# Cross-attention softmax sums: GpSimd adds seven of a head's eight probability chunks instead of six

## The chip, the cores and the metric

The kernel runs on one core of a Trainium2 chip. The metric is the device time of one execution in microseconds (us), as the median of several runs. Engines are named as in the profile: PE is TensorE's matmul queue and PEld its weight loads, DVE is VectorE, ACT is ScalarE, POOL is GpSimd, SP is SyncE, which issues most of the DMAs.

## The reference

Three layers follow each other: a cross-attention of 256 tokens over a context of 4096 rows, a causal self-attention, and a gated feed-forward network. Only the first matters here. It has 16 heads of 32 dimensions:

```python
q = _qdq(x) @ _qdq(wq).T + bq
kv = cond @ wkv.T + bkv
k, v = jnp.split(kv, 2, axis=-1)
# q, k, v reshaped to heads
attn = jax.nn.softmax(jnp.einsum('bnhd,bmhd->bhnm', q, k) * scale, axis=-1)
o = jnp.einsum('bhnm,bmhd->bnhd', attn, v).reshape(B, N, C)
out = _qdq(o) @ _qdq(wp).T + bp
```

So each head needs exponentials of 256 x 4096 scores, their product with V, and, for every token, the sum of its 4096 exponentials, by which the product is divided.

## The kernel before

The program first computes K and V of the context (up to about 207 us), then the 16 heads (to about 466 us), then the projection, the self-attention and the feed-forward network.

A head's 4096 context rows are cut into eight chunks (CHUNKS = 8) of 512. The probabilities of a chunk are stored transposed, context rows on the partitions, as 128 x 1024 float32: four blocks of 128 rows by 256 tokens. They stand in p_ring, which has four places; chunk c lies in place c % 4, so chunk c + 4 overwrites chunk c.

For each head h, the engines do this:

- PE, in `scores` (line 1347): four matmuls a chunk into a PSUM bank pair. Between them `maximum_pass` (line 1254) computes scores of the next head, of which VectorE takes row maxima (line 946).
- ACT, in `exponentials` (line 689): one exponential a chunk, from PSUM to p_ring.
- PE, in `values` (line 1359): the product of a chunk's probabilities with V, summed in bank 6 over the chunks.
- The sum over context rows: a product with a matrix of ones, `denominators` (line 1371), four matmuls into the other half of bank 6. It isn't made for every chunk. Chunks in SUM_CHUNKS are first added to each other elementwise, into p_sum, and one product with ones is made of the result. The others get their own.
- POOL, in `sum_chunks` (line 570), makes these additions for heads 0 to 14: the first adds chunks 0 and 1, each later one adds a chunk to p_sum. p_sum has two places, for even and odd heads. In head 15 DVE does them, in `add_last` (line 1034).
- After the last chunk, PE waits for all additions of the head, makes the product with ones of p_sum, and signals sums_used. ACT then copies bank 6 to o_t, in `evacuate_output` (line 678). `merge` on PE (lines 1333, 1335) and `normalize_output` on DVE divide.

Every engine works through its own queue in program order. The order around the change:

- PE, in `head(h)`, goes through four rounds: maxima, scores of two chunks, maxima, and then the values of the two chunks before these. In the first round of head h those are chunks 6 and 7 of head h - 1, and with chunk 7 comes the product of head h - 1's p_sum. `merge(h - 1)` stands in the second round.
- ACT makes exponential 0 of head h, then copies o_t for head h - 1, and then makes exponentials 1 to 7.

```python
for c in range(CHUNKS):
    if c == 1 and not first:
        evacuate_output(h - 1)           # waits for sums_used, line 677
    act.wait_ge(s_done, 8 * h + c + 1)
    wait(act, pv_done, 8 * h + c - 3)
    summed = SUMS_BEFORE[c]
    if summed is not None:
        wait(act, sums_done, NSUMS * h + summed)
```

SUMS_BEFORE[c] says how many additions, counted from the start of the head (NSUMS a head, negative for the head before), must be over before exponential c may overwrite its place in p_ring; None where the overwritten chunk isn't added. On PE:

```python
if c not in SUM_CHUNKS:
    last = denominators(p_ring[:, c % 4, :])
last.then_inc(pv_done, 1)
if c == CHUNKS - 1:
    pe.wait_ge(sums_done, NSUMS * h + NSUMS)
    denominators(p_sum[:, p, :]).then_inc(sums_used, 1)
```

Of the kernel before, what the change touches and what calls it, by code (L numbers as in the profile page):

```python
# [43 lines left out]
DH = D // H  # L44
HPG = P // DH
SPLIT_ROWS = 3 * DH
SUM_CHUNKS = (0, 1, 2, 4, 5, 6)
NSUMS = len(SUM_CHUNKS) - 1
SUMS_BEFORE = (-2, -1, 0, None, 1, 1, 2, None)
MAX_ROWS = 2  # L50
MT = M // P
CHUNKS = MT // 4
# [52 lines left out]
def wait(eng, sem, value):  # L105
    if positive(value):
        eng.wait_ge(sem, value)


def perceiver(nc, x_in, stream, wq_in, wp_in, bias_cols, bias_rows, out):  # L110
    with ExitStack() as ctx:
# [416 lines left out]
        def _(pool):  # L528
# [33 lines left out]
            def sum_chunks(h, p):  # L562

                for n, c in enumerate(SUM_CHUNKS[1:]):
                    pool.wait_ge(exp_done, 8 * h + c + 1)
# [44 lines left out]
        def _(act):  # L610
# [69 lines left out]
            def exponentials(h, first=False):  # L680
                for c in range(CHUNKS):
# [3 lines left out]
# [3 lines that stand above are left out]
# [173 lines left out]
        def _(dve):  # L861
# [165 lines left out]
            def add_last(n):  # L1027

                h, c = H - 1, SUM_CHUNKS[n + 1]
                dve.wait_ge(exp_done, 8 * h + c + 1)  # L1030
# [168 lines left out]
        def _(pe):  # L1199
# [152 lines left out]
            def values(h, p, loads, c):  # L1352
# [5 lines left out]
                for k in range(4):  # L1358
                    last = nc.tensor.matmul(bank(6)[k * DH:(k + 1) * DH, 0:N], v_head[p][:, 4 * c + k, :],  # L1359
                                            p_ring[:, c % 4, k * N:(k + 1) * N], start=c == 0, stop=c == CHUNKS - 1)  # L1360
                if c not in SUM_CHUNKS:
                    last = denominators(p_ring[:, c % 4, :])
# [5 lines left out]
            def denominators(probabilities):  # L1368

                for k in range(4):  # L1370
                    last = nc.tensor.matmul(bank(6)[k * DH:(k + 1) * DH, N:2 * N], ones_col[:],  # L1371
                                            probabilities[:, k * N:(k + 1) * N], start=False, stop=False,
                                            skip_group_check=True)
                return last
# [292 lines left out]
```

## Time and profile before

| | |
|---|---|
| median of 3 runs | 666.28 us (665.68 to 669.96) |
| the profiled execution | 667.73 us, span 665.9 us |
| PE busy | 618.1 us, 93% of the span |
| DVE busy | 372.9 us, 56% |
| ACT busy | 298.4 us, 45% |
| POOL busy | 228.2 us, 34% |
| mean granted TensorE clock | 0.972 of full speed |

The span is the time from the first to the last instruction of the profiled execution. Busy time of an engine is the time in which an instruction of it runs. The 34% of POOL lie mostly between 209 and 452 us; in the stretch before it does nearly nothing. In a timeline, a row can stand for several instructions in a row; its second number is then the time from the start of the first to the end of the last. A bracket gives the idle time of the engine before the row and what ended it.

### The profile page before, as it was taken

What the parts mean: (1) busy time and instruction counts of PE and PEld (TensorE: products, weight loads), DVE (VectorE), ACT (ScalarE), POOL (GpSimd) and SP (SyncE); (2) the same over time, 40 slices, a digit from 0 to 9 for tenths busy, and PEclk for the clock granted to TensorE, in tenths of its full rate; (3) what the DMA queues carried; (4) which work ended last, traced back from release to release, by engine and by line L of the source; (5) the groups of instructions that cost most, each with busy time, mean ns of one, the idle gap of its engine ahead of it and who ended that gap; (6) DMA issues with size and microseconds to landing.
All of it is one profiled execution on the core that took longest, in us unless ns stands there. A gap on an engine that the chain in (4) does not pass through costs nothing.

```text
span 665.9 us, 12397 instructions
## 1 busy us (share of the span) xinstructions
PE 618.1 (93%) x4340; PEld 478.0 (72%) x4340; DVE 372.9 (56%) x680; ACT 298.4 (45%) x424; POOL 228.2 (34%) x120
## 2 busy tenths in 40 slices
PE   5999999999998999999999999998499899979998
PEld 3877788888885666666666666665289788769997
DVE  3796530332237777777777777754555333365552
ACT  3444233133324444444555555554236676744441
POOL 1000200000024777767777777771100544320000
PEclk9999999999999999999999999997689799979999
DMA  8673644443386555555555555520022224135520
GB/s 305 231 242 126 200 147 167 157 161 120 127 253 178 139 140 138 138 138 138 138 138 138 138 138 142 143 79 1 0 83 109 85 105 189 65 120 186 184 81 32
DMA packets 29757, 92.17 MB, mean 138 GB/s; under 512 B 5472, under 2 KB 9568, under 8 KB 23008
## 3 DMA queue, kind: packets, MB, share of 16 engines
q1 hardware_dynamic: 28480, 89.67, 44.5%
q10 hardware_dynamic: 1248, 2.10, 0.8%
q8 instruction: 19, 0.31, 0.2%
q14 instruction: 10, 0.08, 0.0%
HBM read 65.02 MB, written 18.35 MB: 125 GB/s over the span
## 4 chain that ended last, share of the span: by engine, by line
PE 83%; ACT 6%; DVE 5%; issue 3%; DMA 2%; POOL 1%; SPq 0%; ACTq 0%; POOLq 0%; DVEq 0%
PE ps L333 16%; PE ps L334 15%; PE ps L335 15%; PE ps L1254 10%; PE ps L1359 9%; PE ps L1347 8%; PE ps L1371 3%; ACT p_ring L689 3%; POOL p_sum L570 1%; PE ps L1333 1%; PE ps L1335 1%; DMA f_ring<-stream 1%; DMA k_stack<-kh_scratch 1%; PE ps L1496 1%; PE ps L1325 1%
## 5 line engine op out<-in xcount | busy, mean ns | idle before, releaser
L946 DVE TENSOR_REDUCE m_part<-ps 128x1 f32<-128x512 f32 (+1 forms) x256 | 165.5, 686 | 93.0 <-PE ps L1254 87.4
L689 ACT ACTIVATE p_ring<-ps 128x1024 f32<-128x1024 f32 x128 | 124.6, 1024 | 100.9 <-PE ps L1347 100.9
L570 POOL TENSOR_TENSOR p_sum<-p_sum,p_ring 128x1024 f32<-128x1024 f32 x60 | 142.8, 2380 | 11.6 <-ACT p_ring L689 7.5
L1254 PE MATMUL ps<-k_stack,q_max 96*128 96x512 f32 (+1 forms) x256 | 98.3, 438 | 3.6 <-DVE m_part L946 1.3
L1347 PEld LDWEIGHTS ps<-q_stack,k_stack 98*128 98x128 f32 x512 | 71.2, 191 | 18.6 <-ACT p_ring L689 11.0
L1347 PE MATMUL ps<-q_stack,k_stack 98*128 98x256 f32 x512 | 77.0, 289 | 7.8 <-ACT p_ring L689 7.8
L1359 PE MATMUL ps<-p_ring,v_head 128*32 128x256 f32 x1024 | 75.4, 390 | 0.1
L1254 PEld LDWEIGHTS ps<-k_stack,q_max 96*128 96x128 f32 x256 | 42.6, 188 | 42.7 <-issue 21.2
L333 PE MATMUL ps<-xt_h,h_ring 128*128 128x256 f32 x208 | 61.0, 293 | 2.2 <-DVE xt_l L1060 2.2
L334 PE MATMUL ps<-xt_l,h_ring 128*128 128x256 f32 x208 | 60.5, 291 | 0.0
L335 PE MATMUL ps<-xt_h,l_ring 128*128 128x256 f32 x208 | 60.4, 290 | 0.0
L333 PE MATMUL ps<-h_ring,wkv_h 128*128 128x512 f32 x128 | 52.2, 408 | 8.5 <-DVE l_ring L866 8.1
L906 DVE SCALAR_TENSOR_TENSOR kl_buf<-ps,biases,kh_buf 128x512 fp32r<-128x512 f32 x32 | 23.9, 749 | 63.6 <-ACT kh_buf L647 63.3
L570 POOL TENSOR_TENSOR p_sum<-p_ring 128x1024 f32<-128x1024 f32 x15 | 35.6, 2372 | 67.8 <-ACT p_ring L689 67.8
L312 DVE TENSOR_TENSOR l_ring<-f_ring,h_ring 128x2048 fp32r<-128x2048 f32 x22 | 50.2, 2288 | 12.6 <-ACT h_ring L308 12.5
L334 PE MATMUL ps<-l_ring,wkv_h 128*128 128x512 f32 x128 | 51.5, 402 | 0.0
L335 PE MATMUL ps<-h_ring,wkv_l 128*128 128x512 f32 x128 | 51.5, 402 | 0.0
L333 PE MATMUL ps<-wkv_h,h_ring 128*128 128x512 f32 x128 | 50.8, 397 | 0.0
L335 PE MATMUL ps<-wkv_h,l_ring 128*128 128x512 f32 x128 | 50.6, 396 | 0.0
L334 PE MATMUL ps<-wkv_l,h_ring 128*128 128x512 f32 x128 | 50.6, 395 | 0.0
L661 ACT COPY v_all<-ps 128x512 f32 (+1 forms) x32 | 18.8, 587 | 69.3 <-PE ps L335 69.3
L647 ACT ACTIVATE kh_buf<-ps,biases 128x512 fp32r<-128x512 f32 x32 | 22.0, 688 | 57.2 <-PE ps L335 57.2
(183 smaller groups left out, 1016.6 us busy)
## 6 DMA issues: line engine op xcount, KB each, us to landing
f_ring<-stream SPq DMA_DIRECT2D x29, 1024.0 KB, 4.9
k_stack<-kh_scratch SPq DMA_DIRECT2D x60, 256.0 KB, 4.6
kh_scratch<-kh_buf SPq DMA_DIRECT2D x32, 256.0 KB, 5.5
kl_scratch<-kl_buf SPq DMA_DIRECT2D x32, 256.0 KB, 5.9
v_head<-v_all SPq DMA_DIRECT2D x16, 512.0 KB, 3.0
k_stack<-kl_scratch SPq DMA_DIRECT2D x30, 256.0 KB, 4.2
v_all<-stream SPq DMA_DIRECT2D x4, 256.0 KB, 4.7
f_ring<-stream SPq DMA_DIRECT2D x4, 256.0 KB, 5.7
```

The costliest lines, as they stand in the source:

```text
L312: nc.vector.tensor_tensor(l_ring[which][:], f_ring[which][:], h_ring[which][:].bitcast(F32), ALU.subtract).then_inc(l_ready, 1)
L333: nc.tensor.matmul(out_ap, lh, rh, start=start, stop=False)
L334: nc.tensor.matmul(out_ap, lh, rl, start=False, stop=False)
L335: return nc.tensor.matmul(out_ap, ll, rh, start=False, stop=stop)
L570: nc.gpsimd.tensor_tensor(p_sum[:, p, :], p_ring[:, 0, :] if n == 0 else p_sum[:, p, :], p_ring[:, c % 4, :], ALU.add).then_inc(sums_done, 1)
L647: nc.scalar.activation(kh_buf[:, g, :], bank(g % 2), ACT.Identity, bias=biases[:, KT + g:KT + g + 1]).then_inc(kh_evac, 1)
L689: nc.scalar.activation(p_ring[:, c % 4, :], ps[:, 2 * (c % 2):2 * (c % 2) + 2, :].rearrange("p b n -> p (b n)"), ACT.Exp, scale=XSCALE).th ...
L906: nc.vector.scalar_tensor_tensor(out=kl_buf[:, g, :], in0=bank(g % 2), scalar=biases[:, KT + g:KT + g + 1], in1=kh_buf[:, g, :].bitcast(F3 ...
L946: nc.vector.reduce_max(m_part[:, mc0 + j // NT, j % NT:j % NT + 1], bank(4 + j % 2), AX.X).then_inc(max_read, 1)
L1254: nc.tensor.matmul(bank(to), q_max[p][0:SPLIT_ROWS, at128(j % NT)], k_stack[p][0:SPLIT_ROWS, k_at], start=True, stop=True).then_inc(max_do ...
L1347: last = nc.tensor.matmul(ps[:, 2 * (c % 2) + k // 2, (k % 2) * N:(k % 2 + 1) * N], k_stack[p][0:SPLIT_ROWS + MAX_ROWS, at128(4 * c + k)], ...
L1359: last = nc.tensor.matmul(bank(6)[k * DH:(k + 1) * DH, 0:N], v_head[p][:, 4 * c + k, :], p_ring[:, c % 4, k * N:(k + 1) * N], start=c == 0 ...
```

## The change

SUM_CHUNKS gets chunk 3, so it has seven chunks, and NSUMS goes from 5 to 6. In heads 0 to 14 POOL makes six additions of 128 x 1024 float32 instead of five, in head 15 DVE does, each in the order of the chunks. PE makes no product with ones of chunk 3; those of chunk 7 and of p_sum stay. The exponential of chunk 7, which overwrites chunk 3, now also waits for the third addition. The other entries of SUMS_BEFORE keep their numbers.

```diff
-SUM_CHUNKS = (0, 1, 2, 4, 5, 6)
+SUM_CHUNKS = (0, 1, 2, 3, 4, 5, 6)
 NSUMS = len(SUM_CHUNKS) - 1
-SUMS_BEFORE = (-2, -1, 0, None, 1, 1, 2, None)
+SUMS_BEFORE = (-2, -1, 0, None, 1, 1, 2, 3)
```

## Rows read from the trace of the kernel before

**Rows 1.** The page, busy time of each engine over the whole span

```profile
PE 618.1 (93%) x4340; PEld 478.0 (72%) x4340; DVE 372.9 (56%) x680; ACT 298.4 (45%) x424; POOL 228.2 (34%) x120
```

**Rows 2.** Waits, 209 to 440 us: who waited for whom, total, times, longest

```profile
POOL p_sum L570 <- ACT p_ring L689: 74.9, 29, 15.0
...
ACT o_t L678 <- PE ps L1371: 26.4, 14, 1.9
```

**Rows 3.** Windows between first additions, first and last of 14: stretch, length, busy times, clock

```profile
209.22:225.87 16.65, 15.70 (x146) 10.28 (x146) 12.55 (x23) 8.43 (x10) 11.90 (x6) 1.00 0.49 121
...
422.89:439.22 16.33, 15.80 (x149) 10.65 (x149) 12.03 (x26) 8.27 (x10) 11.90 (x6) 1.00 0.55 142
```

**Rows 4.** Timeline of one steady head, 340 to 358 us: start, length, what

```profile
340.06 2.89 ACT L689 ACTIVATE p_ring<-ps 128x1024 f32<-128x1024 f32 x3
...
341.25 2.37 POOL L570 TENSOR_TENSOR p_sum<-p_ring 128x1024 f32<-128x1024 f32 x1 [3.65 <-ACT p_ring L689]
...
345.40 1.94 ACT L689 ACTIVATE p_ring<-ps 128x1024 f32<-128x1024 f32 x2 [2.45 <-PE ps L1347]
...
346.58 7.30 POOL L570 TENSOR_TENSOR p_sum<-p_sum,p_ring 128x1024 f32<-128x1024 f32 x3 [0.50 <-ACT p_ring L689]
...
349.15 1.94 ACT L689 ACTIVATE p_ring<-ps 128x1024 f32<-128x1024 f32 x2 [1.81 <-PE ps L1347]
...
352.95 1.02 ACT L689 ACTIVATE p_ring<-ps 128x1024 f32<-128x1024 f32 x1 [1.86 <-PE ps L1347]
...
354.54 0.35 PEld L1371 LDWEIGHTS ps<-p_ring,ones_col 128*32 128x32 f32 x8
...
354.97 0.34 PEld L1371 LDWEIGHTS ps<-p_sum,ones_col 128*32 128x32 f32 x8
...
355.87 0.58 ACT L678 COPY o_t<-ps 128x512 f32<-128x512 f32 x1 [1.89 <-PE ps L1371]
...
357.45 2.37 POOL L570 TENSOR_TENSOR p_sum<-p_ring 128x1024 f32<-128x1024 f32 x1 [3.57 <-ACT p_ring L689]
```

**Rows 5.** The instructions of line 570: duration in ns, least, median, greatest

```profile
L570 POOL TENSOR_TENSOR p_sum<-p_sum,p_ring x60: 2358/2382/2394, 211.7 to 449.6; 128x1024 f32<-128x1024 f32 x60
L570 POOL TENSOR_TENSOR p_sum<-p_ring x15: 2367/2372/2383, 209.2 to 439.2; 128x1024 f32<-128x1024 f32 x15
```

**Rows 6.** Timeline from head 14 to head 15, 444 to 464 us

```profile
444.54 7.41 POOL L570 TENSOR_TENSOR p_sum<-p_sum,p_ring 128x1024 f32<-128x1024 f32 x3 [0.42 <-ACT p_ring L689]
...
452.00 0.16 PEld L1371 LDWEIGHTS ps<-p_sum,ones_col 128*32 128x32 f32 x8 [1.43 <-POOL p_sum L570]
...
452.71 0.59 ACT L678 COPY o_t<-ps 128x512 f32<-128x512 f32 x1 [2.51 <-PE ps L1371]
...
454.26 1.23 DVE L1034 TENSOR_TENSOR p_sum<-p_ring 128x1024 f32<-128x1024 f32 x1 [6.11 <-ACT p_ring L689]
...
460.93 2.55 DVE L1034 TENSOR_TENSOR p_sum<-p_sum,p_ring 128x1024 f32<-128x1024 f32 x2 [2.85 <-ACT p_ring L689]
```

**Rows 7.** Windows of 2 us, 450 to 462 us: PE, PEld, DVE, ACT, POOL, clock

```profile
450.00:452.00 2.00, 1.05 (x20) 0.39 (x12) 0.00 (x0) 0.21 (x1) 1.95 (x1) 1.00 0.00 0
452.00:454.00 2.00, 1.31 (x12) 0.69 (x12) 0.00 (x0) 1.29 (x2) 0.00 (x0) 1.00 0.00 0
454.00:456.00 2.00, 1.72 (x10) 1.72 (x10) 1.27 (x2) 1.83 (x3) 0.00 (x0) 0.64 0.00 0
456.00:458.00 2.00, 2.00 (x20) 1.27 (x20) 1.90 (x5) 0.33 (x1) 0.00 (x0) 0.50 0.06 12
458.00:460.00 2.00, 2.00 (x14) 1.44 (x7) 0.08 (x1) 0.18 (x1) 0.00 (x0) 0.50 0.00 0
460.00:462.00 2.00, 2.00 (x23) 1.10 (x26) 1.07 (x1) 1.76 (x2) 0.00 (x0) 0.65 0.00 0
```

**Rows 8.** Timeline of POOL, the last three additions of heads 0 and 1

```profile
214.38 7.41 POOL L570 TENSOR_TENSOR p_sum<-p_sum,p_ring 128x1024 f32<-128x1024 f32 x3 [0.24 <-ACT p_ring L689]
...
231.20 7.44 POOL L570 TENSOR_TENSOR p_sum<-p_sum,p_ring 128x1024 f32<-128x1024 f32 x3 [0.42 <-ACT p_ring L689]
```

## Prediction

> **What bounds the kernel now.** I read the page's busy shares first [rows 1]: TensorE (PE) is busy in 93% of the span and GpSimd (POOL) in 34%, so an exchange of TensorE work for GpSimd work looks cheap. These are averages over the whole program, though. The sixteen attention heads fill only the stretch from about 207 to 466 us, and all of the change lies there. So the next view was the list of waits for the stretch of heads 0 to 13 [rows 2]. ScalarE waits 26.4 us, 1.9 us each time, for the ones-products (line 1371) before it copies o_t, and GpSimd waits 74.9 us for exponentials, which includes 15.0 us before its first addition; nobody is seen waiting for GpSimd. The windows cut at each head's first addition [rows 3] give the head's length: from 209.22 to 439.22 us there are 14 heads, 230.0 us, 16.43 us a head, and PE is busy for 15.7 to 15.8 us of it. PE sets the pace of these heads. GpSimd is busy 11.90 us of each: five additions of 2.38 us.
>
> The timeline of one head [rows 4] shows who hands over to whom, and that matters more than the shares. The head's first addition begins at 341.25, the last three end at 346.58 + 7.30 = 353.88. PE begins to load the weights for the ones-products of p_sum at 354.97. GpSimd is thus only 1.09 us early. Then comes a chain on which the next head depends: ones-products, the copy of o_t (355.87), the exponential of chunk 1 queued behind this copy on ScalarE, and the next head's first addition at 357.45, since it adds chunks 0 and 1. The two engines therefore form a ring: GpSimd's additions, then this closing leg, then GpSimd's additions again. Today the ring has slack where PE arrives later than the last addition.
>
> **The change, part by part.**
>
> *Removed on TensorE.* Four matmuls with ones for chunk 3 of each head (eight records). In the rows the ones-products of chunk 7 start loading at 354.54 and those of p_sum, the next in the queue, at 354.97 [rows 4]: a group costs 0.43 us. A head that PE alone set would take 16.43 - 0.43 = 16.00 us. The matmuls of values stay, and ones-products of p_sum and of chunk 7 stay.
>
> *Added on GpSimd.* One addition a head for heads 0 to 14, of the same form as the 60 that add to p_sum: 2.38 us, with a spread of 2.358 to 2.394 us only [rows 5]. Between successive ones a little more passes: three additions take 7.30 us [rows 4], so their starts lie (7.30 - 2.38) / 2 = 2.46 us apart. In heads 0, 1 and 14, three take 7.41 to 7.44 us [rows 6, 8], or 2.52 us from start to start; these heads lie outside GpSimd's loop, and I keep their own figure. Are the six additions of a head fed in time? The exponentials of chunks 1 to 3 come in one run that ends at 342.95; chunks 4 and 5 are there at 347.34 and chunks 6 and 7 at 351.09 [rows 4]. Additions started every 2.46 us from 341.25 would want chunk 3 at 346.17, chunk 4 at 348.63, chunk 5 at 351.09 and chunk 6 at 353.55. All are there, so from the first to the last GpSimd has no gap. A head's additions take 5 x 2.46 + 2.38 = 14.68 us in the loop and 5 x 2.52 + 2.38 = 14.98 us in the three others.
>
> *The new wait.* The last addition ends at 341.25 + 14.68 = 355.93. PE, now 0.43 us earlier, wants the sum at 354.54: 1.39 us too early. It stands there in order, so the next maxima and scores wait behind it, ScalarE's copy of o_t waits for the ones-products, and the exponential of chunk 1 waits behind the copy. The lost time isn't caught up later, because GpSimd's next round starts only after this exponential.
>
> *The closing leg.* From the end of the last addition to the first addition of the next head. The steady heads can't show it directly, because PE is late there. The change from head 14 to 15 does, where PE really waited for GpSimd [rows 6]: the additions end at 444.54 + 7.41 = 451.95, PE loads at 452.00, the copy starts at 452.71 and the first addition of head 15 (VectorE's there) at 454.26, so 2.31 us. From copy to addition it is 1.55 us there, but 357.45 - 355.87 = 1.58 us in the steady head with GpSimd as the receiver [rows 4]; with that the leg is 2.34 us. The upper bound is the steady head's own leg, 357.45 - 354.97 = 2.48, plus the 0.05 us from the sum to PE: 2.53 us. PE has matmuls in its pipeline there that it wouldn't have after a stall, so I take a value near the lower bound, 2.38 us. The bounds are 2.31 and 2.53.
>
> *A head after the change:* 14.68 + 2.38 = 17.06 us in the loop, 17.36 us in heads 0 and 1. GpSimd and the handing over set it, with PE short of work for 17.06 - 16.00 = 1.06 us in each. Heads 0 to 13 take 12 x 17.06 + 2 x 17.36 = 239.4 us instead of 230.0: **+9.4 us**.
>
> *Head 14.* There is no head 16 whose maxima PE could compute, PE waits for GpSimd already, and the additions ended 451.95 - 439.22 = 12.73 us after the first had begun. With six they take 14.98: **+2.25 us**, all of it on the path.
>
> *Head 15.* VectorE adds here. The sixth addition costs 1.2 us (460.93: two take 2.55 us), but VectorE stood idle for 2.85 us ahead of the fourth chunk's exponential [rows 6], and chunk 3's addition fits in there: nothing. If the idle time were not there it would be 1.2 us. PE's group for chunk 3 goes away: **-0.4 us**.
>
> *Moved waits.* The exponential of chunk 7, which overwrites chunk 3, now waits for the third addition. It ends at 341.25 + 2 x 2.46 + 2.38 = 348.55, and the exponential of chunk 7 starts at about 349.15 - 0.43 + 0.93 = 349.65: nothing, with 1.1 us in hand. The next head's exponential 0 (352.95 - 0.43) waits for the addition of chunk 4, over at 351.01: nothing. No DMA and no queue of SP is touched; loads of K get more time than before.
>
> *Sum:* 9.4 + 2.25 - 0.4 = +11.2 us. The profiled execution took 667.73 us (span 665.9 and 1.8 around it) and would take 678.9. It lies 1.45 us above the median of the runs, 666.28, from which I forecast **677.5 us**, 1.7% slower.
>
> **The clock after a stall.** Around the wait of head 14, PE was busy for 1.05 and 1.31 us of two stretches of 2 us. [...] After the change each head has a stall of 1.4 us, and a shorter one at its heels while PE waits for the exponential of chunk 1. That is nearly as idle as the place where the clock fell, but over the whole head PE's busy share stays near (15.7 - 0.4) / 17.06 = 0.90. [...] In head 14 the stall grows from 1.43 us to 1.43 + 2.25 + 0.43 = 4.1 us; a fall there is in the time of before already, so I take no change, with 3.4 us either way as bounds (that it goes away, or comes twice).
>
> [...]
>
> **Rivals.**
> 1. *The addition is hidden (the other side).* PE stays the bound and 0.43 us a head is won: 16 x 0.43 = 6.9 us, 659.4 us. For it speaks GpSimd's share, 11.90 of 16.43 us, with 4.5 us a head idle. Against it: the idle time is the closing leg and can't be filled. It decides where six additions and the leg fit in 16.00 us: an addition every (16.00 - 2.38) / 6 = 2.27 us, and none of 75 took under 2.358. Chance 0.03. Between this and the forecast, with the leg short enough to lose under 1% (less than 6.7 us, a head of 16.7 us or less), 0.06.
> 2. *The clock falls in the heads.* [...] A fall changes where the next stall lies, so a few are likelier than all. For it: the row at 454 us. Against: all windows of heads 0 to 13 that I read hold 1.00, with some 0.5 to 0.9 us of idle time on PE in each [rows 3]. Chance of four or more 0.10.
> 3. *GpSimd's additions slow down when they run without a pause.* If all heads have 2.52 us from start to start, it is 12 x 0.3 = 3.6 us more, 681.1 us. It is inside my range. Chance 0.08.
>
> **How the numbers follow.** The forecast (ring of GpSimd and the closing leg, 17.0 to 17.2 us a head) gets 0.73. Its bounds: leg of 2.31 or 2.53 us, 14 x -0.07 = -1.0 or 14 x 0.15 = +2.1; the clock beside head 14, -3.4 or +3.4; additions at 2.52, +3.6. That spans 673.1 to 686.6, and up to three or four falls of the clock end at the same place. The range is 673 to 687. About 1% (6.7 us) is what a measurement of this kernel can tell from no change. Slower by over 1% needs over 672.9 us: the forecast and rivals 2 and 3, 0.91. Within 1%: 0.06. Faster: 0.03.
>
> **What would show it.** Right: the windows between first additions are 17.0 to 17.2 us; PE's ones-products of p_sum carry a wait for GpSimd in about 15 heads, 1.2 to 1.5 us each (some 20 us in total with head 14's); GpSimd's six additions stand in one unbroken run, and its idle time before the next is 2.3 to 2.5 us. Wrong: waits for GpSimd of much under 1 us (rival 1), a granted clock of 0.50 in slices of heads 0 to 13 (rival 2), or a gap between additions, which would mean that an exponential comes late.

## The result and the profile after

The changed kernel takes 681.14 us (677.91 to 685.47, four executions), against 666.41 us before; the ratio is 1.020, with a 95% interval of 1.015 to 1.026. In a second series on another occasion (e1_after, below) the ratio was 1.015, interval 1.009 to 1.020. It is slower, by 14.7 us in the first series and by 11.3 us in the second. The forecast was 677.5 us, slower, in a range of 673 to 687.

The executions of either kernel differ by some microseconds with the mean granted clock (of the changed one, 677.91 us at 0.972 and 685.47 us at 0.959). What follows compares the profiled execution of after, 677.91 us (span 676.1), with that of before, 667.73 us (span 665.9); both had a mean clock of 0.972.

The page of after, its busy shares; it answers to [rows 1]:

```profile
PE 613.7 (91%) x4212; PEld 472.1 (70%) x4212; DVE 373.9 (55%) x681; ACT 298.7 (44%) x424; POOL 263.7 (39%) x135
```

PE lost 128 records and 4.4 us of busy time (16 heads of eight records each), POOL got 15 additions and 35.5 us. VectorE and ScalarE are as before. The shares show what work moved, but not where the time went.

The waits of after, 209 to 455 us, answer to [rows 2]. A row says who waited for whom, the total, how often, and the longest:

```profile
POOL p_sum L570 <- ACT p_ring L689: 48.4, 15, 15.0
ACT o_t L678 <- PE ps L1371: 35.9, 14, 2.7
PEld ps L1371 <- POOL p_sum L570: 13.4, 14, 1.1
...
PE ps L1254 <- DMA k_stack<-kh_scratch: 5.9, 12, 0.9
```

The third row is the new wait: TensorE stands for GpSimd in front of the ones-products of p_sum in 14 heads, 0.96 us on average. Behind it, ScalarE waits 35.9 instead of 26.4 us for its copy. The fourth row was 1.2 us before; it wasn't in the forecast.

The timeline of after, from one head to the next, answers to [rows 4] (start, length, what, idle time before it and who ended it):

```profile
346.25 2.38 POOL L570 TENSOR_TENSOR p_sum<-p_ring 128x1024 f32<-128x1024 f32 x1 [2.43 <-ACT p_ring L689]
...
348.71 12.21 POOL L570 TENSOR_TENSOR p_sum<-p_sum,p_ring 128x1024 f32<-128x1024 f32 x5
...
352.88 0.73 PE L1254 MATMUL ps<-k_stack,q_max 96*128 96x512 f32 x2 [0.42 <-DMA k_stack<-kh_scratch]
...
359.55 0.34 PEld L1371 LDWEIGHTS ps<-p_ring,ones_col 128*32 128x32 f32 x8
...
360.97 0.16 PEld L1371 LDWEIGHTS ps<-p_sum,ones_col 128*32 128x32 f32 x8 [1.08 <-POOL p_sum L570]
...
361.68 0.59 ACT L678 COPY o_t<-ps 128x512 f32<-128x512 f32 x1 [2.69 <-PE ps L1371]
...
363.27 2.38 POOL L570 TENSOR_TENSOR p_sum<-p_ring 128x1024 f32<-128x1024 f32 x1 [2.35 <-ACT p_ring L689]
```

The five later additions follow without a gap: 348.71 + 12.21 = 360.92. PE loads at 360.97, 0.05 us after, and GpSimd starts its next round at 363.27. Its idle time, 2.35 us, is the closing leg, and the head is 17.02 us long. This is the ring, closed.

The windows between first additions, answering to [rows 3] (length, then busy time of PE, PEld, DVE, ACT, POOL, the clock, the DMA share and GB/s); the first is a head outside GpSimd's loop, the second and third are in it, the fourth goes from head 14's first addition to head 15's:

```profile
226.56:243.97 17.41, 15.69 (x141) 10.39 (x142) 12.12 (x26) 8.37 (x10) 14.25 (x7) 1.00 0.53 137
346.25:363.27 17.02, 15.51 (x141) 10.19 (x141) 11.93 (x26) 8.19 (x10) 14.28 (x7) 1.00 0.53 135
431.38:448.38 17.00, 15.58 (x141) 10.27 (x141) 12.03 (x26) 8.27 (x10) 14.26 (x6) 1.00 0.52 132
448.38:465.64 17.26, 12.70 (x130) 8.51 (x130) 5.68 (x17) 8.22 (x10) 14.23 (x6) 0.97 0.00 1
```

### The profile page after: what moved, and what is told of

It is laid out like the page before. It is cut to its first block, busy times and chain, and to the rows that moved or that the text cites. A ratio compares the mean times of both kernels' runs of the same rounds, so it can differ in the third digit from the quotient of the medians.

```text
span 676.1 us, 12199 instructions
## 1 busy us (share of the span) xinstructions
PE 613.7 (91%) x4212; PEld 472.1 (70%) x4212; DVE 373.9 (55%) x681; ACT 298.7 (44%) x424; POOL 263.7 (39%) x135
## 4 chain that ended last, share of the span: by engine, by line
PE 53%; issue 25%; POOL 10%; DVE 5%; ACT 4%; DMA 1%; POOLq 1%; SPq 0%; ACTq 0%; DVEq 0%
PE ps L333 16%; PE ps L334 15%; PE ps L335 15%; POOL p_sum L570 10%; ACT p_ring L689 2%; PE ps L1371 1%; PE ps L1254 1%; PE ps L1347 1%; DMA f_ring<-stream 1%; PE ps L1496 1%; PE ps L1359 1%; PE ps L1509 1%; DVE m_part L946 0%; ACT qt_h L722 0%; DVE pt_l L1060 0%
## 5 line engine op out<-in xcount | busy, mean ns | idle before, releaser
L570 POOL TENSOR_TENSOR p_sum<-p_sum,p_ring 128x1024 f32<-128x1024 f32 x75 | 178.2, 2376 | 6.9
L689 ACT ACTIVATE p_ring<-ps 128x1024 f32<-128x1024 f32 x128 | 124.7, 1024 | 99.8 <-PE ps L1347 96.8
L560 POOL MEMSET k_stack<- 32x4096 f32 x1 | 3.5, 3517 | 118.2 <-PE ps L335 118.2
```

Of the source, the lines that this page charges most:

```text
L570: nc.gpsimd.tensor_tensor(p_sum[:, p, :], p_ring[:, 0, :] if n == 0 else p_sum[:, p, :], p_ring[:, c % 4, :], ALU.add).then_inc(sums_done, 1)
L689: nc.scalar.activation(p_ring[:, c % 4, :], ps[:, 2 * (c % 2):2 * (c % 2) + 2, :].rearrange("p b n -> p (b n)"), ACT.Exp, scale=XSCALE).th ...
```

## The experiments

Two theories stood against each other. *The ring*: the sixth addition closes the ring of additions and closing leg, and only its length and the place of the copy matter. *The load*: six additions are too much for GpSimd as such, or their traffic or the new wait of exponential 7 costs. Beside it stood a question that the new DMA wait raised: what was the removed work on TensorE worth? I read every profile at one place more than the total, the time from head 2's first addition to head 14's, twelve heads. Before it is 196.74 us, after 204.41:

```profile
242.48:439.22 196.74, 189.55 (x1777) 127.54 (x1777) 144.25 (x301) 99.13 (x109) 142.69 (x61) 1.00 0.55 140
243.97:448.38 204.41, 187.08 (x1681) 123.22 (x1681) 144.14 (x300) 99.16 (x109) 171.09 (x72) 1.00 0.53 135
```

**The change again (e1_after).** No edit.

> The changed kernel again, beside the experiments. Ring theory: about 678 to 685 us, and the executions with the lower mean TensorE clock are the longer ones (below 0.965 where the time is over 682 us). Rival (the executions differ for another reason than the clock): time and mean clock don't go together.

Six executions: 678.23 to 683.98 us, median 679.71, ratio 1.015 (1.009 to 1.020). Time and mean clock go together: 678.2 us at 0.972, 679.4 to 680.0 at 0.970 to 0.971, 683.7 and 684.0 at 0.959. The profiled one is one of the long ones, 683.65 us. Its windows of 3 us at the start of the heads (the clock is the third number from the end):

```profile
204.00:207.00 3.00, 2.17 (x8) 0.91 (x7) 2.92 (x5) 0.00 (x0) 0.00 (x0) 0.88 0.94 242
207.00:210.00 3.00, 3.00 (x12) 2.54 (x11) 1.29 (x2) 1.28 (x2) 0.00 (x0) 0.50 0.65 232
210.00:213.00 3.00, 2.55 (x8) 1.85 (x8) 2.58 (x4) 0.66 (x1) 2.17 (x1) 0.50 0.00 0
213.00:216.00 3.00, 3.00 (x22) 1.57 (x21) 1.29 (x2) 1.94 (x2) 2.06 (x2) 0.50 0.43 117
```

The clock fell where the heads begin, ahead of any new wait. The twelve heads take 451.33 - 246.90 = 204.43 us in it, the same as in the short execution. Of the 5.7 us between the two spans, 2.9 lie before these heads (246.90 against 243.97) and the other 2.8 behind them. So the spread between these two doesn't come from the stalls in the heads.

**The copy moved (e2_after_copy2), and the same on the kernel before (e3_before_copy2).**

```diff
-                    if c == 1 and not first:
+                    if c == 2 and not first:
                         evacuate_output(h - 1)
```

> The changed kernel, with ScalarE's copy of o_t put behind the exponential of chunk 1 instead of ahead of it. Ring theory: GpSimd's next round no longer waits for the ones-products and the copy, six additions (14.7 us) fit into a head, PE sets the pace again at 15.5 to 16.0 us a head, and the kernel takes 650 to 661 us, less than before the change. Rival (six additions are themselves too much for GpSimd, or disturb other engines, or the new wait of exponential 7 costs): it stays above 672 us.

> The kernel before (five additions), with the copy put behind the exponential of chunk 1. Both theories: only PE's 0.5 us gap ahead of the fourth chunk's scores goes away in each head, so 657 to 664 us. Ring theory: the changed kernel with the same edit is 4 to 7 us faster than this one, which is what the removed ones-products are worth (16 x 0.43 us); the rival has it slower than this one.

With seven chunks: 666.44 us, ratio to before 0.997 (0.993 to 1.000). With six: 662.53 us, ratio 0.991 (0.987 to 0.995). So 13 us of the loss are gone with one comparison changed, although GpSimd makes as many additions as in the changed kernel. That speaks for the ring and against the load. It isn't below 661 us as expected, though, and the kernel with seven chunks is 4 us slower than its partner, not faster. These are two findings. The 4 us don't lie in the twelve heads, which take 193.73 us, the partner's 194.30. In the two profiles, head 14 is 1.0 us longer with seven chunks (15.82 and 14.83 us), and all that follows head 15's first addition is 3.8 us longer (213.59 and 209.82 us, with mean clocks of 0.90 and 0.93): behind head 14's wait of 2.87 us the clock fell with seven chunks (0.50 from 452 to 458 us), and behind one of 1.44 us with six it didn't (1.00 from 454 to 468 us). That is one profile of each, so it isn't shown for the medians. The other finding is that the twelve heads gain only 0.6 us, while PE has 12 x 0.43 = 5.2 us less to do. The timeline of the kernel with seven chunks shows what PE does instead:

```profile
331.27 0.72 PE L1254 MATMUL ps<-k_stack,q_max 96*128 96x512 f32 x2 [0.76 <-DMA k_stack<-kh_scratch]
```

These maxima are the first of the head after next. They need the first half of its K, whose load can only be issued after the scores of chunk 3, as the buffer is free then; issued at 325.54 to 326.41, it lands 4.0 us later. The ones-products of chunk 3 had stood between the two.

**TensorE's work kept (e4_keep_ones).**

```diff
-                if c not in SUM_CHUNKS:
+                if c not in SUM_CHUNKS or c == 3:
```

> The changed kernel, but TensorE makes the ones-products of chunk 3 as before (chunk 3 counts twice in the denominators). Ring theory: PE has 1.06 us in hand in each head, the 0.43 us go into its wait for GpSimd, and the time is that of the changed kernel within 0.5% or a little less, as there is less idle time that could lower the clock. Rival (PE's own work still sets the heads): 6 to 7 us more.

682.15 us, ratio 1.020 (1.012 to 1.027), beside 1.015 (1.009 to 1.020) of the changed kernel on the same chip: these intervals overlap. The twelve heads take 204.53 us, and took 204.41 without the products. So the added 5.2 us of PE work in them cost 0.1 us: inside the ring, PE has this time in hand.

**TensorE's work taken away alone, in two places (e5_drop_ones, e11_drop_ones7).** Both on the kernel before, with five additions.

```diff
-                if c not in SUM_CHUNKS:
+                if c not in SUM_CHUNKS and c != 3:      # e5; in e11: c != 7
```

> The kernel before, with only TensorE's ones-products of chunk 3 taken away (chunk 3 is missing in the denominators, GpSimd makes five additions as before). First theory, PE alone sets the heads: 16 x 0.43 = 6.9 us less, ratio 0.990. Second theory, the load of K's first half for the head after next (issued after the scores of chunk 3, used by the maxima that stood 0.43 us behind it) lands no earlier and turns the saving into a wait: 0 to 3 us less, ratio 0.995 to 1.000, with a wait of PE line 1254 for the DMA k_stack of 0.3 us or more in most heads.

> The kernel before, with only the ones-products of chunk 7 taken away (chunk 7 is missing in the denominators, five additions as before). Same 0.43 us of PE work as taking away chunk 3's, but in another place: directly ahead of the ones-products of p_sum, on which the copy, exponential 1 and the next additions wait. If the place decides: 5 to 7 us less than before, ratio 0.990 to 0.993. If PE's work is worth nothing in any place: ratio 0.998 to 1.003, as without chunk 3's.

Without chunk 3's products the ratio is 1.003 (0.999 to 1.007): no gain. Without chunk 7's it is 0.992 (0.988 to 0.997), 664.87 us, 4.3 us less. The same four matmuls a head are worth 0.04 us a head in one place (twelve heads in 196.22 us) and 0.50 us in the other (190.79 us). Why, says the list of waits of e5, 225 to 430 us:

```profile
PE ps L1254 <- DMA k_stack<-kh_scratch: 6.0, 12, 0.9
```

Before, all of them together were 1.2 us there. Nearly all of PE's saved 5.2 us went into the load of K.

**The K load earlier (e9_after_copy2_early_k, e10_before_copy2_early_k).** K's first half is loaded as two quarters with semaphores of their own, the first of them two chunks earlier. Both kernels also have the moved copy.

```diff
-                for half in range(2):
-                    sp.wait_ge(s_done, 8 * h + 4 * half + 4)
+                for half, chunks in enumerate((2, 4, 8)):
+                    sp.wait_ge(s_done, 8 * h + chunks)
                     load_k(p, h + 2, half)
...
-                    if j % 8 == 0:
-                        pe.wait_ge(ks_loaded[p][j // 8], 48 * (loads - 1 + p))
+                    if j in (0, 4, 8):
+                        pe.wait_ge(ks_loaded[p][j // 4], 48 * (loads - 1 + p))
```

> The changed kernel with the copy behind the exponential of chunk 1, and with K's first half loaded as two quarters, the first already after the scores of chunk 1. Theory of the late K load: PE's wait of 0.76 us a head for the DMA goes away, 14 x 0.7 = 10 us less than the same kernel without it: 654 to 659 us. If it is not the load that limits, nothing changes (663 to 669).

> The kernel before with both of these edits. It has 0.43 us of ones-products a head more on PE, so if PE sets the pace in both, this one is 6 us longer in heads 0 to 13 and 2.2 us shorter behind head 14, so 3 to 5 us slower than its partner with seven chunks: 657 to 662 us.

With seven chunks 660.36 us, ratio 0.988 (0.981 to 0.995); with six 656.23 us, ratio 0.983 (0.977 to 0.989). The DMA wait is gone with seven chunks and is down to 0.8 us in all with six, and the heads are shorter: twelve in 188.71 and in 188.79 us. So the late load was real, but the removed products still gain nothing, 0.1 us in twelve heads. The 4.1 us between the two medians lie elsewhere again: in the profiles, 1.0 us in head 14 and 3.2 us behind head 15's first addition (212.37 and 209.14 us), where the clock fell beside head 14 with seven chunks only (0.50 from 446 to 452 us, and 1.00 from 444 to 458 us with six). The same place in both timelines, with seven chunks first:

```profile
327.41 0.22 DVE L994 TENSOR_REDUCE a_part<-o_all  x1
327.79 2.58 DVE L946 TENSOR_REDUCE m_part<-ps 128x1 f32<-128x512 f32 x4 [0.15 <-DVE a_part L994]
...
328.53 0.19 PEld L1254 LDWEIGHTS ps<-k_stack,q_max 96*128 96x128 f32 x1 [0.27 <-DVE m_part L946]
```

```profile
327.62 0.21 DVE L994 TENSOR_REDUCE a_part<-o_all  x1
...
327.98 2.68 DVE L946 TENSOR_REDUCE m_part<-ps 128x1 f32<-128x512 f32 x4 [0.15 <-PE ps L1254]
```

VectorE has its small work between two heads there (the head's maximum and a_part, 0.9 us). With chunk 3's products PE's maxima come just as it is done, and it waits for PE; without them they come too early, and PE waits for VectorE. So a second cover stands behind the first, at the same place. It isn't GpSimd: with seven chunks no engine waits for it in heads 1 to 13. No run moved VectorE's small work, so this cover is read from the timelines and not tested. The expected sign between the two kernels was wrong because the gain in the heads that it counted on is missing. The one with six chunks is the fastest kernel of this study, 1.7% under the kernel before.

**The size of the sixth addition (e6_half, e7_quarter3, e12_seventh).** The first two shorten chunk 3's addition, the third adds chunk 6 twice.

```diff
+                    w = 512 if c == 3 else CW               # e6; in e7: 768
-                    nc.gpsimd.tensor_tensor(p_sum[:, p, :], p_ring[:, 0, :] if n == 0 else p_sum[:, p, :],
-                                            p_ring[:, c % 4, :], ALU.add).then_inc(sums_done, 1)
+                    nc.gpsimd.tensor_tensor(p_sum[:, p, 0:w], p_ring[:, 0, :] if n == 0 else p_sum[:, p, 0:w],
+                                            p_ring[:, c % 4, 0:w], ALU.add).then_inc(sums_done, 1)
...
-SUM_CHUNKS = (0, 1, 2, 3, 4, 5, 6)                          # e12
-SUMS_BEFORE = (-2, -1, 0, None, 1, 1, 2, 3)
+SUM_CHUNKS = (0, 1, 2, 3, 4, 5, 6, 6)
+SUMS_BEFORE = (-3, -2, 0, None, 1, 1, 2, 3)
```

> The changed kernel, with the addition of chunk 3 over 512 of the 1024 columns in heads 0 to 14 (the other half of chunk 3 is missing in the denominators). Ring theory: the ring is about 1.2 us shorter, 15.9 us a head, and PE or its loads set the pace again at 16.1 to 16.4 us: 14 x 0.7 to 0.9 us plus 1.2 us of head 14 less than the changed kernel, so 665 to 670 us, ratio to the kernel before 0.995 to 1.003. Rival (it is the number of additions or the extra dependency that costs, not their time): near 679 us.

> The changed kernel, with the addition of chunk 3 over 768 of 1024 columns in heads 0 to 14 (a quarter of chunk 3 is missing in the denominators). Ring theory: 17.06 - 0.6 = 16.46 us a head, just above what the other limits give (16.2 to 16.4): 1 to 4 us more than the kernel before, 669 to 673 us. A cost that comes with the addition as such would give the same as the whole addition, near 680.

> The changed kernel with one addition more, chunk 6 twice (it counts twice in the denominators): seven additions a head in heads 0 to 14 on GpSimd, and in head 15 on VectorE. Ring theory: every head is one addition longer, 15 x 2.46 = 37 us more than the changed kernel, 714 to 720 us, ratio 1.07; the idle time of GpSimd between heads stays at 2.3 to 2.5 us. A theory by shares of busy time (GpSimd 14.3 us of 17.1) would have only a part of it. PE would stand for 3.5 us a head, so its clock may fall in the heads; it has that time in hand, and the time then wouldn't change.

| addition of chunk 3 | time, us | ratio to before | twelve heads, us | a head, us |
|---|---|---|---|---|
| none (the kernel before) | 668.39 to 669.24 | 1 | 196.74 | 16.40 |
| 512 columns | 669.97 | 1.001 (0.998 to 1.005) | 196.04 | 16.34 |
| 768 columns | 675.36 | 1.007 (1.003 to 1.012) | 197.92 | 16.49 |
| 1024 columns (the changed kernel) | 679.71 | 1.015 (1.009 to 1.020) | 204.41 | 17.03 |
| and a seventh addition | 729.57 | 1.086 (1.082 to 1.090) | 245.89 | 20.49 |

The ratios are each to the runs of the kernel before in the same series. The loss has a threshold. Half an addition is free: the ring would be 15.9 us, and the other limits give 16.34; GpSimd is idle for 2.6 to 3.1 us between heads. At 768 columns this idle time is down to the closing leg, 2.35 and 2.44 us by turns, so the ring is closed. It is just the longest, 16.49 us a head against 16.46 expected, and from there it goes one for one: 256 columns more are 0.54 us more a head (expected 0.6). The total of e7 missed its bounds of 669 to 673; its median execution had a clock of 0.962, and those with 0.972 took 671.4 and 671.6.

The seventh addition missed by 10 us: 50 us more than the changed kernel, not 37. TensorE's clock did it. PE waits for GpSimd ahead of each head, and the clock falls to 0.50 in 12 of heads 1 to 14. Ahead of nine of these the wait was 1.48 to 1.60 us, ahead of the other three 2.75, 3.38 and 3.24 us. Ahead of heads 6 and 11, in which the clock held, it was 0.92 and 0.93 us. The windows of 3 us in one head with a fall:

```profile
294.00:297.00 3.00, 3.00 (x13) 2.81 (x13) 1.29 (x3) 1.76 (x2) 2.92 (x2) 0.50 0.31 88
297.00:300.00 3.00, 3.00 (x21) 1.62 (x21) 0.58 (x3) 0.00 (x0) 2.92 (x2) 0.50 0.78 178
300.00:303.00 3.00, 3.00 (x29) 1.99 (x27) 2.48 (x4) 1.82 (x2) 1.85 (x2) 0.90 0.00 0
```

I had written that this wouldn't cost, since PE has the time in hand. It has it at the end of the head. The slow stretch lies at its start, where PE makes the scores of chunks 4 and 5, and GpSimd runs dry:

```profile
301.18 1.94 ACT L689 ACTIVATE p_ring<-ps 128x1024 f32<-128x1024 f32 x2 [5.02 <-PE ps L1347]
...
302.36 2.39 POOL L570 TENSOR_TENSOR p_sum<-p_sum,p_ring 128x1024 f32<-128x1024 f32 x1 [1.15 <-ACT p_ring L689]
```

So 1.1 to 1.5 us of GpSimd's idle time stand inside the ring in most heads. Where the clock held, the two heads took 19.83 us (335.32 to 355.15) and 19.90 us, near 17.03 + 2.46 = 19.49; the other ten of the twelve took 20.47 to 20.87 us. The 0.3 to 0.4 us more than 19.49 stand in GpSimd's idle time behind them, 2.79 and 2.87 us, as the clock falls again there.

**The wait filled (e8_fill).**

```diff
+                    if not (isinstance(h, int) and h == H - 1):
+                        for _ in range(2):
+                            for k in range(4):
+                                nc.tensor.matmul(bank(7)[k * DH:(k + 1) * DH, N:2 * N], ones_col[:],
+                                                 v_all[:, 0, 0:8, :], start=True, stop=True,
+                                                 skip_group_check=True)
                     pe.wait_ge(sums_done, NSUMS * h + NSUMS)
```

> The changed kernel, but PE fills 0.86 us of its wait for GpSimd in each of heads 0 to 14 with matmuls whose result nobody reads. Ring theory: the time is that of the changed kernel within 0.5%, 677 to 683 us. If the stalls lower PE's clock in the heads and so make the kernel slower in some executions, the spread of the executions shrinks and the median falls by 2 us or more.

685.3 us (680.0 to 689.2), ratio 1.023 (1.016 to 1.030). Nothing gets steadier or faster: two executions had a clock of 0.972, the others 0.955 and 0.959. The twelve heads take 206.09 us, 1.7 more than the changed kernel's, or 0.14 us a head. That fits what e5_drop_ones says PE had in hand, 17.03 - 16.35 = 0.68 us a head, of which 0.86 us of filling takes 0.18 too much; the prediction had counted 1.06. The falls of the clock seen in e1_after lie outside the filled heads, and filling is no remedy here.

## Why the prediction was right, and where it was off

**The ring.** This is what was predicted, and each of its terms has its row. Additions of a head in the loop: 2.46 + 12.21 = 14.67 us (predicted 14.68). Closing leg: GpSimd is idle for 2.35 and 2.43 to 2.45 us by turns (predicted 2.38, taken between 2.31 and 2.53 from [rows 4, 6]). Its choice near the lower bound was right for the reason given: from PE's load to the copy it is 361.68 - 360.97 = 0.71 us, as behind the stall of head 14 before, and not the 0.90 us of the steady head before. Head: 17.03 (17.06). Heads 0 and 1: 243.97 - 209.22 = 34.75 us for both (34.72). The experiments show the cause: moving the copy by one exponential removes the loss, half an addition costs nothing, and a whole one costs what the ring is then longer than the other limits, 17.03 - 16.35 us.

**The sum.** Heads 0 to 13 +9.2 us (9.4), head 14 14.95 instead of 12.73 us, +2.2 (2.25), and from head 15's first addition to GpSimd's first instruction of the next stage 14.08 instead of 14.93 us, -0.85 (-0.4, the least exact of the terms). Together 10.5; the spans differ by 10.2, as the rest is 0.3 us shorter. For this execution 678.9 us had been worked out, and it took 677.9.

**The median** is 681.1, 3.6 us above the forecast. The executions above it had mean clocks of 0.967 and 0.959; the one long profile (e1_after) has its slow stretches at the start of the heads and behind them. The time differs in this way from one execution to the next in both kernels (before: 664.5 to 674.0 us in the three later series), and the median of four or six executions carries it; the forecast was made from an execution with a mean clock of 0.972. So how close the median comes is in part luck: the difference between the medians was 14.7 us in the first series and 11.3 us in the second, with 11.2 predicted. That the changed kernel suffers more from the clock was not shown.

**Off: the head that PE alone would set.** The step was "a head that PE alone set would take 16.43 - 0.43 = 16.00 us". Taken alone (e5) it takes 16.35. The 0.43 us lay ahead of maxima that wait for K's first half, and behind that load VectorE's small work covers the same spot (e9 against e10). So rival 1, with a gain of 6.9 us were the addition hidden, had the wrong price: with the ring open (e2 against e3, e9 against e10) the removed products gained 0.6 and 0.1 us in twelve heads. The sum itself wasn't touched, as it took the head from the ring. For the same reason the wait for GpSimd was 0.6 to 1.1 us in heads 0 to 13 instead of 1.2 to 1.5, and 17.5 us in all with head 14's 4.1 instead of some 20: in the head shown, 0.42 of the predicted 1.39 us is the wait for the DMA in front of it. "Loads of K get more time than before" was wrong: none is issued differently, but in front of K's first half 0.43 us of cover is gone.

**Off: the wait of exponential 0** of the next head was said to cost nothing, with a margin of 1.5 us. In head 14, without maxima for PE, ScalarE does wait 1.08 us for GpSimd there. GpSimd sets that head anyway, so it cost nothing.

**The clock in the range.** The range has 3.4 us either way for the clock beside head 14. No run shows that a fall costs this; it can only be estimated, from the granted clocks of 454 to 462 us in [rows 7], as 2 x (0.36 + 0.50 + 0.50 + 0.35) = 3.4 us at the full clock that were not granted. In its place the runs showed that the changed kernel has one fall there too (0.68, 0.50, 0.50 and 0.62 in the four stretches of 2 us from 464 to 472 us), and that behind head 15's first addition a profile with a fall there is 3.8 us longer than one without in one pair (e2_after_copy2, e3_before_copy2) and 3.2 us in the other (e9_after_copy2_early_k, e10_before_copy2_early_k). The clocks of the later stages differ in both pairs too, so neither is the cost of one fall alone.

**Rival 2, the clock.** In the changed kernel no window of heads 1 to 13 fell below 1.00, in either of its two profiles, with stalls of up to 1.1 us and 0.5 us a head. In e12_seventh, with waits of mostly 1.5 us and up to 3.4, it fell in 12 of 14. A head with a fall took 20.47 to 20.87 us there, the two without one 19.83 and 19.90, so 0.6 to 1.0 us more. What the three or four falls that the range also holds would cost the changed kernel, no run shows. Rival 3 (2.52 us from start to start in all heads) fell: in the loop five additions take 12.18 to 12.21 us, 2.45 from start to start.

## What to carry to other kernels

Before work is moved to an idle engine, follow what its last result releases and when its next round may start. If both lie on one loop, its idle share isn't free time, and the limit is its work plus the handing over. Work removed from the busiest engine is worth what stands directly behind it: look for the next wait after that place, for each engine and each load, before its duration enters a sum. And a copy that isn't urgent shouldn't stand in a queue ahead of the instruction that feeds the next round.

## What was not expected of the hardware

In e12_seventh, where PE's wait for GpSimd is 1.5 us in most heads, the clock falls to 0.50 in 12 of 14 of them, and costs time (0.6 to 1.0 us a head) on an engine that seemed off the path, since it delays the early part of a head. After waits of 0.92 and 0.93 us in the same kernel it held, and in the changed kernel waits of up to 1.13 us in heads 0 to 13 leave it at 1.00. The length of the wait alone doesn't settle it: beside head 14 the clock fell to 0.50 behind a wait of 1.43 us in the kernel before, and stayed at 1.00 for the next 14 us behind 1.44 us in e3_before_copy2 and e10_before_copy2_early_k. Two executions of one program differ by up to 9 us (before: 664.5 and 674.0 us, with mean clocks of 0.979 and 0.961); where the slow stretches lie was seen in profiles only, for the changed kernel at the start of the heads and in the stages behind them.
